# TensorE loads 16 numbers of the block table where it loaded 24: a half-width block's index is the end of its expert's full blocks

## What is computed

```python
x = x + _L0_xattn_ref(_layernorm(x), ctx, ctx, mask, wq, bq, wk, bk, wv, bv, wo, bo)
x = x + _L0_ffn_ref(_layernorm(x), gate_w, wg, wu, wd)
x = x + _L1_xattn_ref(_layernorm(x), ctx, ctx, fside, fside, fside, Wq, bq, Wk, bk, Wv, bv, ...)
x = x + _L1_ffn_ref(_layernorm(x), Wg, W1, W2)
```

## Time and profile before

| | |
|---|---|
| three runs | 899.75, 907.44, 909.17 us (median 907.44) |
| the profiled execution | 902.42 us, span from first to last instruction 900.6 us |
| TensorE busy with matmuls | 706.9 us (78%) |
| TensorE busy with weight loads (beside them) | 554.4 us (62%) |
| VectorE, ScalarE, GpSimd busy | 558.0, 403.7, 290.9 us |
| mean granted TensorE clock | 0.880 |
| share of the chain that ended last | TensorE 48%, VectorE 22%, "issue" 10%, ScalarE 8%, DMA 6% |

### The profile page before, as it was taken

How to read it: one execution, slowest core, us unless ns; L and a number is a source line. 1 busy time by engine, 2 the same in 40 slices (tenths; PEclk the granted TensorE clock), 3 DMA queues, 4 the chain that set the end, 5 groups by cost and what they waited for, 6 DMA issues and landing times.

```text
span 900.6 us, 19126 instructions
## 1 busy us (share of the span) xinstructions
PE 706.9 (78%) x6266; PEld 554.4 (62%) x6278; DVE 558.0 (62%) x1394; ACT 403.7 (45%) x720; POOL 290.9 (32%) x285
## 2 busy tenths in 40 slices
PE   5676787987753899999997999995771199889982
PEld 4323444553543789989896899985440077667771
DVE  7778586877663544757555647559788246556441
ACT  1136465666630434645545546443342054535431
POOL 7415202416158121221122122220055314423442
PEclk9789798979676899999999999996655599999997
DMA  4661301501536342526435636224032645554332
GB/s 138 125 141 40 59 1 45 151 30 48 151 109 216 110 111 40 165 43 164 128 81 154 172 53 168 40 38 164 24 120 90 212 119 123 129 118 122 59 57 40
DMA packets 68419, 92.26 MB, mean 102 GB/s; under 512 B 14442, under 2 KB 54435, under 8 KB 68348
## 3 DMA queue, kind: packets, MB, share of 16 engines
q1 hardware_dynamic: 41788, 63.37, 23.8%
q0 software_dynamic: 14592, 16.24, 10.3%
q10 hardware_dynamic: 11968, 11.72, 5.0%
HBM read 64.21 MB, written 29.87 MB: 104 GB/s over the span
## 4 chain that ended last, share of the span: by engine, by line
PE 48%; DVE 22%; issue 10%; ACT 8%; DMA 6%; ACTq 2%; POOL 2%; DVEq 0%; POOLq 0%; SPq 0%
PE ps L657 45%; DVE probs L1688 2%; DVE mx L1552 2%; DMA out_x<-keys,row_to 2%; DMA probs<-rows 2%; DVE stats L1356 2%; DVE keys L1766 2%; ACT probs L1162 1%; POOL rows L610 1%; PE ps L905 1%; DVE probs L1771 1%; ACT expo L1159 1%; ACT probs L1244 1%; DVE keys L1745 1%; ACT xln L1109 1%
## 5 line engine op out<-in xcount | busy, mean ns | idle before, releaser
L1766 DVE TENSOR_TENSOR keys<-probs,ps 128x512 f32<-128x512 f32 x122 | 82.8, 687 | 181.4 <-PE ps L657 101.1
L657 PE MATMUL ps<-keys,slot 128*128 128x256 f16 (+1 forms) x1440 | 148.5, 265 | 5.6 <-DVE keys L1745 2.9
L657 PEld LDWEIGHTS ps<-keys,slot 128*128 128x128 f16 x1440 | 128.8, 100 | 24.1 <-issue 5.7
L657 PE MATMUL ps<-keys,probs 128*128 128x256 f16 (+1 forms) x1488 | 139.2, 255 | 5.5 <-DVE probs L1366 3.8
L657 PEld LDWEIGHTS ps<-keys,probs 128*128 128x128 f16 x1488 | 124.1, 98 | 19.2 <-issue 7.5
L573 POOL DMA_INDIRECT attended<-keys,row_to x42 | 65.7, 1565 | 169.4 <-ACT keys L1253 141.1
L1240 ACT ACTIVATE probs<-ps 128x512 f32<-128x512 f32 x122 | 71.6, 598 | 69.0 <-PE ps L657 66.2
L1253 ACT ACTIVATE keys<-ps,carried 128x256 f32<-128x256 f32 x80 | 33.5, 470 | 120.9 <-PE ps L657 43.3
L1771 DVE TENSOR_TENSOR probs<-keys,probs 128x512 f16<-128x512 f32 x122 | 83.2, 687 | 3.6 <-ACT probs L1244 1.7
L1244 ACT CAST probs<-keys 128x512 f16<-128x512 f32 x122 | 74.8, 614 | 21.7 <-DVE keys L1766 21.7
L1688 DVE TENSOR_TENSOR probs<-expo,probs 128x512 f16<-128x512 f32 x80 | 62.0, 786 | 33.6 <-ACT probs L1162 33.4
(11 more groups left out here) (276 smaller groups left out, 1173.9 us busy)
## 6 DMA issues: line engine op xcount, KB each, us to landing
inbox<-in_W SPq DMA_DIRECT2D x24, 512.0 KB, 5.1
probs<-rows ACTq DMA_DIRECT2D x44, 260.0 KB, 2.8
inbox<-in_wg SPq DMA_DIRECT2D x16, 512.0 KB, 5.5
inbox<-in_wu SPq DMA_DIRECT2D x16, 512.0 KB, 4.8
inbox<-in_wd SPq DMA_DIRECT2D x16, 512.0 KB, 3.9
rows<-zeros SPq DMA_DIRECT2D x16, 260.0 KB, 2.4
x<-in_x SPq DMA_DIRECT2D x4, 512.0 KB, 6.4
q_out<-queries SPq DMA_DIRECT2D x8, 256.0 KB, 2.1
```

Of the source, the lines that this page charges most:

```text
L657: return pe.matmul(o, l, r, start=start, stop=stop, **kw)
L1766: dve.tensor_tensor(h32[:, j % 2, :], s_act[:, j % 2, :], ps[:, 2 * (j % 2) + 1, :], ALU.mult).then_inc(S(r + "_h32"), 1)
```

## The change

VectorE no longer writes `TB_LAST`, and TensorE no longer loads it. Where a half-width block exists, `room` is 1 and `full_end` = `blk_end` - 1 is that block's index, so it is taken from there. The upper limit of the assertion on `full_ends` becomes `MAXBLK - 1`.

```diff
-TB_FULL, TB_LAST = 64, 80
+TB_FULL = 64
...
                 pe.wait_ge(S(r + "_table"), 1)
-                lasts = [pe.value_load(tb[0:1, TB_LAST + e:TB_LAST + e + 1], min_val=0, max_val=MAXBLK - 1) for e in range(E)]
                 ends = [0] + [pe.value_load(tb[0:1, e:e + 1], min_val=1, max_val=MAXBLK) for e in range(1, E + 1)]
-                full_ends = [pe.value_load(tb[0:1, TB_FULL + e:TB_FULL + e + 1], min_val=0, max_val=MAXBLK) for e in range(E)]
+                full_ends = [pe.value_load(tb[0:1, TB_FULL + e:TB_FULL + e + 1], min_val=0, max_val=MAXBLK - 1) for e in range(E)]
...
                     with pe.If(end - full_end):
-                        one_block(lasts[e], wh, wl, P)
+                        one_block(full_end, wh, wl, P)
...
-                ch(dve.tensor_scalar(tb[0:1, TB_LAST:TB_LAST + E], be, -1.0, None, ALU.add))
                 ch(dve.tensor_tensor(tb[0:1, TB_FULL:TB_FULL + E], be, room[:, :], ALU.subtract))
```

## The result

The changed kernel takes 898.34 us (median of 20 runs, 892.16 to 902.98), the kernel before 908.05 us (median of 20, 899.75 to 911.6). The ratio is 0.9897, with a 95% interval of 0.9875 to 0.9918: 9.4 us less, between 7.4 and 11.3. The forecast was 898.0 us and a gain of 8.8.

What follows compares the result with a forecast made beforehand. TensorE's table-number loads ahead of each layer's first expert transposes were taken as the bound. 5.2 us (layer 0) plus 3.6 (layer 1) made 8.8 off the 907.44 median, 898.6, given as 898; range 889 to 905.

Steps and rivals of the forecast that it cites:

- The holes are the loads: TensorE's "issue" waits at line 905, 38.3 us over both layers, are its 24 table-number loads queued ahead of the transposes.
- Layer 0, 5.2 us: Layer 0's hole: sixteen remaining numbers end at 289.0, after the rows at 288.11, so transposes start 5.2 us sooner.
- the price follows SyncE's reads and not the line: TensorE's early loads are dear because SyncE reads the table then; deleting line 948's loads saves 5.2 us, not 7.2.
- Layer 1, 3.6 us: Layer 1's hole: numbers ready at 711.1, rows landing at 713.32 bound the start; gain 3.6 us, remaining 2.3 worth nothing.
- VectorE's instruction and the other register: nothing: One 0.16 us table instruction fewer, table signalled about 0.08 us earlier, and the half-width block's index from another register: worth nothing.
- The clock: After each hole the return to full clock, 7.1 and 7.6 us after the restart, moves with the start and costs nothing.
- the first rival: The clock returns at the old times, leaving 8.8 us more at half speed: gain 4.4, time 903.0 us; chance 0.13.
- The expert stages as long as before: From the first transposes on, each layer's experts take as long as before; later row and weight fetches stay hidden.
- it doesn't do what it says: Rival: the hole is something else, such as the branch and first instructions; gain 0 to 2, about 906.4 us; chance 0.06.
- slower: Rival: the clock stays at half in layer 1 long after the restart; 918.6 us with 40 us more; chance 0.04.
- more than the sum: Rival: layer 0 gains 6.0 and the clock returns up to 1 us sooner; gain 10.6, time 896.8 us; chance 0.14.

Runs made afterwards that it cites:

- before_rows_sooner: The kernel before (24 numbers), with ScalarE fetching the first block's rows from row 0 outright instead of loading the row from the table: 908.38 against 908.9 us, ratio 0.9989.

## Why the prediction was right

**The holes are the loads.** Right. With 32, 24 and 16 numbers line 905 starts right behind the last one wherever the rows have landed.

| kernels, by numbers ahead | table to line 905, layer 0 | layer 1 |
|---|---|---|
| 32 | 26.9 us | 23.6 us |
| 24 (three traces each) | 20.5 to 21.9 | 18.2 to 18.7 |
| 16, the changed kernel (three traces) | 15.5 to 16.2 | 14.3 to 14.6 |
| 8 | 14.5 | 14.7 |
| 2 | 14.5 | 14.3 |

The last two lines are the floor that the rows set. The first two give the slope: 5.0 to 6.4 us for eight numbers in layer 0, 4.9 to 5.4 in layer 1, where 0.65 us a number makes 5.2.

**Layer 0, 5.2 us.** 5.0 in the pair of traces, 5.0 in the time of the run with this layer alone. The step "the price follows SyncE's reads and not the line" holds as far as it says that the price follows SyncE's loop; that it is the reads is not shown, and SyncE's ten loads that were dear with no other engine reading speak against reads alone. That the numbers are the bound there held in three of four traces; in the one of after it was the rows, by 0.6 us, with the same outcome. The three 24-number traces against the three of the changed kernel give 21.2 - 15.7 = 5.5.

**Layer 1, 3.6 us.** 3.8 in the pair; the means of three traces each give 18.5 - 14.5 = 4.0. That the rows are late next held in each trace. The time of layer 1 alone fell by 2.6 us, with 3.6 well inside its interval.

**VectorE's instruction and the other register: nothing.** Nothing contradicts it. It wasn't tried by itself, since 0.08 us can't be measured in a time. In the pair of traces the last writing of the table starts 0.37 us after the instruction of line 1672 before, and 0.30 us after the same instruction (line 1671) in the changed kernel.

**The clock.** The return doesn't come at the old time (the first rival) but moves with the start. In the stretches of after (columns as in the earlier trace rows):

```profile
287.80:295.10 7.30, 6.43 (x34) 4.61 (x35) 2.22 (x4) 1.26 (x1) 5.87 (x5) 0.50 0.76 271
295.20:303.00 7.80, 7.80 (x76) 7.00 (x74) 5.54 (x7) 5.93 (x10) 0.00 (x0) 1.00 0.22 59
710.40:714.90 4.50, 3.63 (x21) 2.62 (x22) 1.06 (x4) 0.00 (x0) 0.19 (x1) 0.50 0.86 249
715.00:725.00 10.00, 9.52 (x89) 7.96 (x88) 6.53 (x11) 6.82 (x10) 0.00 (x0) 1.00 0.41 141
```

It is back 7.3 and 4.6 us after the start. I had two such times, 7.1 and 7.6, and gave them 1 us of play; over all 14 traces, 28 restarts, they lie between 4.5 and 7.8 us, with a mean of 6.3. At half speed that is up to 1.6 us for one restart, either way. I sized this term too small: in the pair layer 1's return came 3.0 us sooner after the start than before (4.6 against 7.7), where 1 us was allowed for. It is a part of why one execution says little about the tenths.

**The expert stages as long as before.** Not in the pair, where layer 0's took 3.3 us more, for reasons that `before_rows_sooner` shares; within a group they took the same, or 0.7 us more.

**Sum and ranges.** 8.8 us forecast, 9.4 by the ratio, 8.6 and 10.6 in the two repeats. Of the rivals, "it doesn't do what it says", "slower" and the clock's old time fell; "more than the sum" (10.6) lies inside the interval of 7.4 to 11.3, and the runs don't tell it from the forecast. That the median fell within 0.4 us of the figure given is luck: I had moved 898.6 to 898 for the spread of four runs, and the kernel before took 900 us in two groups and 908 or 909 in the others. What the mechanism forecast is the difference.

## What to carry to other kernels

A number loaded from SBUF into a sequencer's register cost 0.65 us here, 0.9 us in the first eight, while SyncE's clearing loop ran, and it is seen only as "issue" in front of the next instruction; count such loads, and look for what lands next before counting on the whole of them. Price the removal by when the last remaining load ends, not by the one deleted. Loads moved into the steady part of a program are hidden only as far as the sequencer is ahead of its engine there, which was 0.8 us and not the 2.2 us seen elsewhere in the same trace.

## What the runs showed of the hardware that I had not expected

TensorE's table load itself takes 293 to 314 ns in most cases and up to 785 ns while SyncE's loop of loads and clearing transfers runs; SyncE's own in that loop take 514 to 558 ns even where no other engine loads. The clock's return after a restart varies from 4.5 to 7.8 us in the same program. A kernel with eight loads fewer, and faster at the place meant, had a new 2.64 us wait 140 us later in code that was not edited, together with an instruction fetch at its end; it was 5.9 us slower in all. After shortening a program, its whole timeline has to be compared, not just the place of the edit.
